# Product with V split over four quarters of the TensorE array, with scores and mask packed to the 64x64 blocks that are kept

## The chip, the cores and the metric

The kernel runs on one core of one Trainium2 chip. The metric is the device time of one execution in microseconds, the median of several runs.

## The reference

The input x has 16 sequences of 256 tokens with 256 features, 4096 tokens in all. A modulation computed from a small vector gives every sequence its shifts, gains and gates. The first half of the layer is a chunked linear attention with 16 heads of 128 features:

```python
h = layernorm(x) * (1 + ca) + sa
q, k, v = (h @ w.T + b for each of the three weights), 16 heads of D = 128
qn, kn = q and k divided by their norms; gv = softplus(h @ b_w.T + b_b) * v
attn = einsum('bnhid,bnhjd->bnhij', qn, kn)       # inside chunks of C = 64 tokens only
mask = where(j <= i, 1, 0)                        # the decay is exp(0) wherever the mask keeps
out = einsum('bnhij,bnhjd->bnhid', attn * mask, gv)
out = (out * silu(h @ og_w.T)) @ o_w.T + o_b
x = x + ga * out
```

The second half is a mixture of 16 experts (top 6 of them by a softmax) and a shared expert on all tokens, added to x with the gate gb.

## The kernel before

**Tiling.** Tokens lie in 32 tiles of 128, in 8 "supertiles" of 512 tokens. The heads lie in 4 groups of 4. The attention part is a loop of N = 128 steps, one for each pair of token tile and head group (`for n in range(N + 2)` at L928 on TensorE and L1507 on VectorE); four steps (t = 0 to 3) make a supertile with one head group. The expert part is a second loop, of 100 units (`for u in range(2, NU)`, L973), in which nothing of the change occurs.

**One step on TensorE, in order.** `project(i, t, Q)`, side tasks, `project(i, t, K)`, at t = 2 half of the output projection of the previous supertile, `score(n - 1)`, `project(i, t, V)`, the other half of the output projection, `attend(n - 1)`, `turn(n)`, more side tasks, and at t = 1 the four gate products. Side tasks are small pieces of other stages (norms, routing, preparing weights) placed by `plan()` (L68). A projection is six matmuls with a moving operand of 512 columns in the reduced fp32r format (`split_product`, L647: high and low parts of both operands, two halves of the contraction). `turn` (L838) transposes Q and K of the step, four matmuls each.

**Scores.** A 128-token tile has two chunks of 64 tokens, c = 0 and 1. `score` (L855) makes for each head and chunk the 64x64 block k.T @ q: contraction over the 128 features, 64 output partitions (the tokens j), 64 columns (the tokens i). Chunk c goes to output partitions 64c to 64c+63 and to columns 64c to 64c+63 of the head's 128, so that a head fills the two diagonal blocks of a 128x128 square in the PSUM bank `s_ps`. Its off-diagonal blocks are not written by these products. All operands are full fp32, for which the program has two pairs of weight load and matmul for each call.

**Mask.** On VectorE, `mask` (L1431) multiplies the whole bank, 128 partitions by 512 columns, by `causal` (128x128, broadcast over the four heads) into `scores`. `causal` is built once by GpSimd (L576 to L585): an upper triangle of ones with the upper right 64x64 block set to zero.

**Product with V.** `attend` (L869) makes for each head out = v.T @ scores with the whole array: contraction over 128 tokens, 128 output partitions (the features), 128 columns, into the PSUM bank `av_ps`. It waits for the mask, for V scaled by GpSimd (`v_scaled`) and for `gated_done` of the step before, which says that `av_ps` was read.

**After it.** On VectorE, `apply_gate` (L1443) multiplies `av_ps` by the gate into `gated`; ScalarE and VectorE split `gated` into a high and a low part for the output projection. `add_bias(n, V)` (L1421) on VectorE waits for `attended`, because it overwrites a V buffer; so do the copies of turned Q and K on ScalarE wait for `scored`.

**PSUM.** All eight banks are in use: two for projections, `qt_ps`, `kt_ps`, `s_ps`, `av_ps`, `out_ps`, `misc`. In the expert part `s_ps` and `av_ps` hold sums of experts; `down` (L906) waits for `masked` and `gated_done` of the last step before it.

Of the kernel before, what the change touches and what calls it, by code (L numbers as in the profile page):

```python
# [6 lines left out]
ALU = mybir.AluOpType  # L7
# [3 lines left out]
P = 128  # L11
# [12 lines left out]
HG = 4  # L24
NG = NH // HG
CH = 64
# [12 lines left out]
Q, K, V, G, O = range(5)  # L39
# [7 lines left out]
def after(eng, sem, count):  # L47
    if count > 0:
        eng.wait_ge(sem, count)
# [6 lines left out]
def heads(ap):  # L56
    return ap.rearrange("p (h d) -> p h d", d=P)
# [77 lines left out]
def build(nc, x, q_w, q_b, k_w, k_b, v_w, v_b, b_w, b_b, og_w, o_w, o_b, gate_w, w13, w2, sw13, sw2, c, wmod, out):  # L135
    ctx = ExitStack()
    with ctx:
        sb = lambda name, shape, dt=FP32: ctx.enter_context(nc.sbuf_tensor(name, shape, dt))
# [15 lines left out]
        beta = sb("beta", [P, NT, NH])  # L154
        minus_half = sb("minus_half", [P, 2 * HG])
        primed = sb("primed", [P, 1])
        causal = sb("causal", [P, P])


        w_qkv = sb("w_qkv", [P, 2, 3, KC, 2, 512], F32R)  # L160
# [3 lines left out]
        raw = [[sb(f"{n}_sb{b}", [P, HG * P]) for b in range(2)] for n in "qkv"]  # L164
# [3 lines left out]
        inv_norm = [sb(f"inv_norm{b}", [P, 2 * HG]) for b in range(2)]  # L168
        v_scale = [sb(f"v_scale{b}", [P, HG]) for b in range(2)]
        q_t, k_t = sb("q_t", [P, HG * P]), sb("k_t", [P, HG * P])  # L170
        scores = sb("scores", [P, HG * P])
        gate = sb("gate", [P, HG, ST])
        gated = [sb(f"gated{b}", [P, HG, P]) for b in range(2)]
        gated_hi, gated_lo = sb("gated_hi", [P, HG, ST], F32R), sb("gated_lo", [P, HG, ST], F32R)
# [37 lines left out]
        boot_ps = [qt_ps, kt_ps, s_ps, av_ps, qt_ps, kt_ps, s_ps, av_ps, av_ps, qt_ps]  # L212
        boot_before = [0, 0, 0, 0, 1, 2, 3, 4, 8, 0]
        late_wmod = [[work[:, 0:512], work[:, 512:1024]], [acc[:, 1, 0:512], acc[:, 1, 512:1024]]]
        y_ps = [[qt_ps, kt_ps], [s_ps, av_ps]]
        g_ps, u_ps = proj_ps[0], [proj_ps[1], out_ps]

# [354 lines left out]
        @block.gpsimd  # L572
        def _(pool):
            pool.memset(ident, 0.0)
            pool.memset(minus_half[:, :], -0.5)
            pool.memset(causal[:, :], 1.0)  # L576
            pool.memset(prob_ext[:, :, E:E + 2], 2.0).then_inc(made, 1)
            pool.wait_ge(made, 1)
            pool.affine_select(out=ident, in_=ident, compare_op=ALU.not_equal, fill=1.0, base=0,
                               pattern=[[-1, P]], channel_multiplier=1)  # L580
            pool.affine_select(out=causal[:, :], in_=causal[:, :], compare_op=ALU.is_ge, fill=0.0, base=0,
                               pattern=[[1, P]], channel_multiplier=-1).then_inc(made, 1)
            pool.wait_ge(made, 2)
            pool.memset(causal[0:CH, CH:P], 0.0).then_inc(made, 1)
            pool.wait_ge(made, 3)  # L585

            def do(task):
                if task[0] == "stats":
                    v = norm_at[task[1:3]]
                    pool.wait_ge(eps_added, v + 1)  # L590
                    after(pool, xn_done, v)
                    pool.tensor_tensor(rstd[:, :], var_eps[:, :], minus_half[:, 0:TS], ALU.pow).then_inc(rstd_done, 1)
                elif task[0] == "tile" and task[1] == NM - 2 and task[2] == 0:
                    u = nat_at["tile", NM - 1]
                    pool.wait_ge(nat_turned, u - 1)
                    pool.memset(nat[u % 2][:, :], 0.0).then_inc(nat_padded, 1)

            for task in boot:
                do(task)
            for n in range(N):  # L600
                i, t = divmod(n, TS)
                b, s, g = t % 2, supertile(i), group(i)
                for task in side[n, 0]:
                    do(task)
                pool.wait_ge(guard_done, n + 1)
                after(pool, q_scaled, n - 1)
                after(pool, scale_done, n - 1)
                pool.tensor_tensor(inv_norm[b][:, :], guarded[b][:, :], minus_half[:, :], ALU.pow).then_inc(inverted, 1)  # L608
                pool.wait_ge(inverted, n + 1)
                q = heads(raw[Q][b][:, :])  # L610
                pool.tensor_tensor(q, q, inv_norm[b][:, 0:HG].unsqueeze(2).broadcast_to([P, HG, P]), ALU.mult)\  # L611
                    .then_inc(q_scaled, 1)
                after(pool, v_scaled, n - 1)
                pool.wait_ge(beta_ready, s + 1)
                pool.tensor_tensor(v_scale[b][:, :], inv_norm[b][:, HG:2 * HG],
                                   beta[:, s * TS + t, g * HG:(g + 1) * HG], ALU.mult).then_inc(scale_done, 1)
                pool.wait_ge(scale_done, n + 1)
                pool.wait_ge(biased[V], n + 1)
                v = heads(raw[V][b][:, :])
                pool.tensor_tensor(v, v, v_scale[b][:, :].unsqueeze(2).broadcast_to([P, HG, P]), ALU.mult)\  # L620
                    .then_inc(v_scaled, 1)
                for task in side[n, 1]:
                    do(task)
            for u in range(NU):
                for task in late[u]:
                    do(task)
# [1 line left out]

        @block.tensor
        def _(pe):  # L630
            pe.wait_ge(made, 3)


            ORDER = [(w, t) for t in range(2) for w in (Q, K, V)] + [("gate", h) for h in range(HG)] + \
# [220 lines left out]
            def score(n):  # L855
                pe.wait_ge(qt_copied, n)
                pe.wait_ge(kt_copied, n)
                after(pe, masked, n - 1)
                if n == 1:
                    pe.wait_ge(gained, 3)  # L860


                for h in range(HG):
                    for c in range(P // CH):
                        at = slice(h * P + c * CH, h * P + (c + 1) * CH)
                        mm = pe.matmul(s_ps[c * CH:(c + 1) * CH, at], k_t[:, at], q_t[:, at], start=True, stop=True)  # L866
                mm.then_inc(scored, 1)

            def attend(n):  # L869
                pe.wait_ge(masked, n)  # L870
                pe.wait_ge(v_scaled, n)
                after(pe, gated_done, n - 1)
                if n == 1:
                    pe.wait_ge(boot_lo, 10)
                for h in range(HG):
                    at = slice(h * P, (h + 1) * P)
                    mm = pe.matmul(av_ps[:, at], raw[V][(n - 1) % 2][:, at], scores[:, at], start=True, stop=True)  # L877
                mm.then_inc(attended, 1)


# [318 lines left out]
        def _(dve):  # L1199
# [196 lines left out]
            def late_modulation():  # L1396
                dve.wait_ge(mod_turned, 2)
                dve.tensor_copy(mod[:, 4:12, :], s_ps[:, 2 * P:4 * P].rearrange("p (r d b) -> p r d b", r=8, d=2)[:, :, 0, :])\
                   .then_inc(gained, 1)
                dve.wait_ge(made, 3)  # L1400
                dve.wait_ge(gained, 3)
                gain = mod[:, CB * KC:(CB + 1) * KC, :]
                dve.tensor_scalar(gain, gain, 1.0, None, ALU.add).then_inc(gained, 1)
                steps = 4
                for w in (GA, GB):
                    m, s = mod[:, w * KC:(w + 1) * KC, :], sign[:, :, :]
                    dve.wait_ge(gained, steps)
                    dve.tensor_scalar(s, m, 0.0, 2.0, ALU.is_ge, ALU.mult).then_inc(gained, 1)
                    dve.wait_ge(gained, steps + 1)
                    dve.scalar_tensor_tensor(out=m, in0=m, scalar=-1.0, in1=m, op0=ALU.mult, op1=ALU.max).then_inc(gained, 1)  # L1410
                    dve.wait_ge(gained, steps + 2)
                    dve.tensor_scalar(m, m, 0.25, None, ALU.max).then_inc(gained, 1)
                    dve.wait_ge(gained, steps + 3)
                    dve.scalar_tensor_tensor(out=m, in0=s, scalar=-1.0, in1=m, op0=ALU.add, op1=ALU.mult).then_inc(gained, 1)
                    steps += 4
                dve.wait_ge(gained, steps)
                for h in range(KC):
                    dve.tensor_scalar(ga_ob[:, h, :], mod[:, GA * KC + h, :], o_b_sb[:, h:h + 1], None, ALU.mult)\
                       .then_inc(gained, 1)
# [11 lines left out]
            def mask(n):  # L1431
                dve.wait_ge(scored, n)
                after(dve, attended, n - 1)
                dve.tensor_tensor(heads(scores[:, :]), heads(s_ps[:, :]),
                                  causal[:, :].unsqueeze(1).broadcast_to([P, HG, P]), ALU.mult).then_inc(masked, 1)

            def sum_squares(n):
                dve.wait_ge(q_squared, n + 1)
# [4 lines left out]
            def apply_gate(n):  # L1443
                i, t = divmod(n - 1, TS)
                dve.wait_ge(attended, n)
                dve.wait_ge(gate_ready, HG * (i + 1))
                after(dve, gated_hi_done, n - 2)
                after(dve, gated_lo_done, n - 2)
                dve.tensor_tensor(gated[t % 2][:, :, :], heads(av_ps[:, :]), gate[:, :, t * P:(t + 1) * P], ALU.mult)\
                   .then_inc(gated_done, 1)  # L1450

            def lo_part(n):
                i, t = divmod(n - 1, TS)
# [133 lines left out]
```

## Time and profile before

| | us |
|---|---|
| median of 3 runs | 2165.3 (2164.62 to 2166.77) |
| the profiled execution | 2164.84 |
| its span in the trace | 2163.1 |
| TensorE busy | 2135.4 (99%) |
| VectorE busy | 1154.5 (53%) |
| ScalarE busy | 1031.5 (48%) |
| GpSimd busy | 522.2 (24%) |

The profiled execution took 0.5 us less than the median, and its span lacks 1.7 us of its time. In the profile PE is TensorE's matmul side and PEld its weight loads, which overlap the matmuls; DVE is VectorE, ACT ScalarE, POOL GpSimd. The end of a matmul is modelled and lies after the start of the next one, so consecutive matmuls overlap in these rows: what a block of matmuls costs is read from its start to the start of the next block, not from its busy time. `x8` on a row is the number of instructions merged in it.

### The profile page before, as it was taken

The page shows a single profiled execution, that of the slowest core. Times are in us where ns is not written, and L with a number is a line of the kernel's source. Part 1 is how long each engine was busy: PE and PEld are TensorE (multiplying, and loading weights), DVE is VectorE, ACT ScalarE, POOL GpSimd, SP SyncE. Part 2 cuts the span into 40 slices and gives each one's busy share as a digit, 9 for nine tenths or more (in the row PEclk, how much of TensorE's full clock was granted, in tenths as well). Part 3 has the DMA queues.
Part 4 walks back from the last instruction along what each step waited for, and adds up shares of the span by engine and source line. Part 5 has one row for each costly group of instructions (what it writes and reads, how often), then busy time and mean ns, then how long its engine had stood idle before and what let it go on. Part 6 is the DMA issues. An engine that isn't in the chain of part 4 may idle for free.

```text
span 2163.1 us, 36173 instructions
## 1 busy us (share of the span) xinstructions
PE 2135.4 (99%) x12463; PEld 1752.6 (81%) x12463; DVE 1154.5 (53%) x2174; ACT 1031.5 (48%) x3300; POOL 522.2 (24%) x540
## 2 busy tenths in 40 slices
PE   8999999999999999999999999999999999999999
PEld 6778888888888887878888888888888888888887
DVE  6555654555555555555554445555555455545554
ACT  6655664665665665565565453333332333333232
POOL 2433443443443343343343441000000000000000
PEclk9999999999999999999999999999999999999999
DMA  8574443254355354354233221342334234323221
GB/s 264 185 239 133 146 138 123 81 162 139 93 145 159 84 154 136 95 147 142 106 143 113 70 107 49 129 170 98 127 125 149 88 121 156 103 97 113 96 94 63
DMA packets 191892, 274.79 MB, mean 127 GB/s; under 512 B 99184, under 2 KB 132960, under 8 KB 191712
## 3 DMA queue, kind: packets, MB, share of 16 engines
q1 hardware_dynamic: 191712, 272.49, 39.6%
q8 instruction: 101, 1.65, 0.3%
q14 instruction: 79, 0.65, 0.1%
HBM read 214.79 MB, written 57.67 MB: 126 GB/s over the span
## 4 chain that ended last, share of the span: by engine, by line
PE 92%; DVE 3%; ACT 2%; issue 2%; DMA 1%; DVEq 0%; POOL 0%; SPq 0%; ACTq 0%; POOLq 0%
PE proj_ps L651 49%; PE out_ps L651 14%; PE av_ps L877 5%; PE s_ps L866 4%; PE s_ps L924 3%; PE av_ps L924 3%; PE qt_ps L924 3%; PE kt_ps L924 3%; PE qt_ps L847 2%; PE kt_ps L852 2%; DMA head_scr<-stage 1%; PE misc_ps L670 1%; PE out_ps L721 0%; ACT squares L1117 0%; PE misc_ps L679 0%
## 5 line engine op out<-in xcount | busy, mean ns | idle before, releaser
L651 PE MATMUL proj_ps<-w_qkv,h_t 128*128 128x512 f32 x2304 | 618.0, 406 | 10.3 <-DVE q_sb L1428 2.1
L651 PEld LDWEIGHTS proj_ps<-w_qkv,h_t 128*128 128x128 f32 x2304 | 407.9, 188 | 103.3 <-issue 20.2
L651 PE MATMUL proj_ps<-h_t,w_qkv 128*128 128x512 f32 x1800 | 444.2, 391 | 0.3 <-issue 0.2
L651 PEld LDWEIGHTS proj_ps<-h_t,w_qkv 128*128 128x128 f32 x1800 | 335.6, 188 | 70.2 <-issue 1.3
L608 POOL TENSOR_TENSOR inv_norm<-guarded,minus_half 128x8 f32<-128x8 f32 x128 | 209.4, 1636 | 741.9 <-DVE guarded L1441 741.9
L1108 ACT ACTIVATE q_t<-qt_ps 128x512 f32<-128x512 f32 x128 | 76.3, 596 | 303.9 <-PE qt_ps L847 303.4
L651 PE MATMUL proj_ps<-h_t,w_gate 128*128 128x512 f32 x768 | 190.2, 398 | 2.6 <-ACT gate L1131 1.3
L1428 DVE TENSOR_TENSOR v_sb<-proj_ps,bias 128x512 f32<-128x512 f32 x128 | 88.5, 691 | 190.0 <-PE av_ps L877 183.4
L1117 ACT ACTIVATE squares<-q_sb 128x128 f32<-128x128 f32 x512 | 151.4, 297 | 56.9 <-DVE q_sb L1428 52.4
L1428 DVE TENSOR_TENSOR q_sb<-proj_ps,bias 128x512 f32<-128x512 f32 x128 | 88.4, 690 | 165.5 <-PE proj_ps L651 160.7
L651 PEld LDWEIGHTS proj_ps<-h_t,w_gate 128*128 128x128 f32 x768 | 139.8, 188 | 40.2 <-ACT gate L1131 10.7
L1117 ACT ACTIVATE squares<-k_sb 128x128 f32<-128x128 f32 x512 | 151.1, 297 | 19.8 <-DVE k_sb L1428 18.2
L651 PE MATMUL out_ps<-gated_hi,w_out 128*128 128x512 f32 x512 | 158.0, 390 | 0.1
L651 PE MATMUL out_ps<-h_t,w_qkv 128*128 128x512 f32 x594 | 150.9, 389 | 0.0
L1428 DVE TENSOR_TENSOR k_sb<-proj_ps,bias 128x512 f32<-128x512 f32 x128 | 88.4, 690 | 116.1 <-PE proj_ps L651 115.7
L877 PEld LDWEIGHTS av_ps<-scores,v_sb 128*128 128x128 f32 x1024 | 133.9, 191 | 10.7
L1151 ACT ACTIVATE w_gate<-v_sb 128x512 fp32r<-128x512 f32 x100 | 63.2, 632 | 161.8 <-DVE v_sb L1499 161.8
L1151 ACT ACTIVATE w_gate<-squares 128x512 fp32r<-128x512 f32 x100 | 63.2, 632 | 158.8 <-DVE squares L1499 154.6
L620 POOL TENSOR_TENSOR v_sb<-v_sb,v_scale 128x512 f32<-128x512 f32 x128 | 135.6, 1059 | 10.0
L611 POOL TENSOR_TENSOR q_sb<-q_sb,inv_norm 128x512 f32<-128x512 f32 x128 | 135.2, 1056 | 10.0
L877 PE MATMUL av_ps<-scores,v_sb 128*128 128x128 f32 x1024 | 134.7, 274 | 0.0
L651 PEld LDWEIGHTS out_ps<-h_t,w_qkv 128*128 128x128 f32 x594 | 111.5, 188 | 23.5
(216 smaller groups left out, 3174.5 us busy)
## 6 DMA issues: line engine op xcount, KB each, us to landing
w_qkv<-tile_scr SPq DMA_DIRECT2D x100, 768.0 KB, 4.3
w_qkv<-head_scr SPq DMA_DIRECT2D x45, 1024.0 KB, 11.0
head_scr<-stage SPq DMA_DIRECT2D x30, 512.0 KB, 3.8
w_gate<-head_scr SPq DMA_DIRECT2D x15, 1024.0 KB, 4.9
w_out<-head_scr SPq DMA_DIRECT2D x15, 1024.0 KB, 4.9
tile_scr<-stage SPq DMA_DIRECT2D x25, 512.0 KB, 3.1
x_in<-_attn_hidden_states_dram SPq DMA_DIRECT2D x16, 512.0 KB, 6.7
h_scr<-stage SPq DMA_DIRECT2D x16, 512.0 KB, 3.3
```

The lines of the kernel that those rows point to most:

```text
L608: pool.tensor_tensor(inv_norm[b][:, :], guarded[b][:, :], minus_half[:, :], ALU.pow).then_inc(inverted, 1)
L611: pool.tensor_tensor(q, q, inv_norm[b][:, 0:HG].unsqueeze(2).broadcast_to([P, HG, P]), ALU.mult)\
L620: pool.tensor_tensor(v, v, v_scale[b][:, :].unsqueeze(2).broadcast_to([P, HG, P]), ALU.mult)\
L651: mm = pe.matmul(out, w, y, start=(j == 0 and m == 0), stop=(3 * j + m == n - 1))
L847: mm = pe.transpose(qt_ps[:, h * P:(h + 1) * P], raw[Q][b][:, h * P:(h + 1) * P], ident)
L866: mm = pe.matmul(s_ps[c * CH:(c + 1) * CH, at], k_t[:, at], q_t[:, at], start=True, stop=True)
L877: mm = pe.matmul(av_ps[:, at], raw[V][(n - 1) % 2][:, at], scores[:, at], start=True, stop=True)
L924: mm = pe.matmul(y_ps[a][h][:, :], tiles_w[:, w % 4, r, at], y, start=(m == 0 and j == 0), stop=(m == NM - 1 and j == 2))
L1108: act.activation(q_t[:, :], qt_ps[:, :], ACT.Copy).then_inc(qt_copied, 1)
L1117: m = act.activation(squares[:, what, at], raw[what][n % 2][:, at], ACT.Square, accum_out=sumsq[n % 2][:, what * HG + h:what * HG + h + 1])
L1151: act.activation(hid_hi[u % 2], hid[u % 2], ACT.Copy).then_inc(hid_hi_done, 1)
L1428: dve.tensor_tensor(raw[what][t % 2][:, :], proj_ps[at][:, :], bias[:, (i // 2) % 2, what, :], ALU.add)\
```

## The change

`score` puts both chunks of a head in the same 64 columns (partitions 0 to 63 and 64 to 127), so that the scores of four heads fill 256 columns and `s_ps` has its second half free. `causal` becomes two 64x64 triangles one above the other. The mask works on 256 columns. `attend` makes, for each head, half d of V's 64 columns and chunk c, a 64x64 product with contraction over 64 tokens; chunk 0 writes `av_ps`, chunk 1 the second half of `s_ps`. The gate is applied by two instructions, one for each chunk. `score` waits for `gated_done` of the step before.

```diff
--- before.py
+++ after.py
@@ -154,7 +154,7 @@
         beta = sb("beta", [P, NT, NH])
         minus_half = sb("minus_half", [P, 2 * HG])
         primed = sb("primed", [P, 1])
-        causal = sb("causal", [P, P])
+        causal = sb("causal", [P, CH])
 
 
         w_qkv = sb("w_qkv", [P, 2, 3, KC, 2, 512], F32R)
@@ -168,7 +168,7 @@
         inv_norm = [sb(f"inv_norm{b}", [P, 2 * HG]) for b in range(2)]
         v_scale = [sb(f"v_scale{b}", [P, HG]) for b in range(2)]
         q_t, k_t = sb("q_t", [P, HG * P]), sb("k_t", [P, HG * P])
-        scores = sb("scores", [P, HG * P])
+        scores = sb("scores", [P, HG * CH])
         gate = sb("gate", [P, HG, ST])
         gated = [sb(f"gated{b}", [P, HG, P]) for b in range(2)]
         gated_hi, gated_lo = sb("gated_hi", [P, HG, ST], F32R), sb("gated_lo", [P, HG, ST], F32R)
@@ -212,6 +212,8 @@
         boot_ps = [qt_ps, kt_ps, s_ps, av_ps, qt_ps, kt_ps, s_ps, av_ps, av_ps, qt_ps]
         boot_before = [0, 0, 0, 0, 1, 2, 3, 4, 8, 0]
         late_wmod = [[work[:, 0:512], work[:, 512:1024]], [acc[:, 1, 0:512], acc[:, 1, 512:1024]]]
+
+        attended_ps = [av_ps[:, 0:HG * CH], s_ps[:, HG * CH:2 * HG * CH]]
         y_ps = [[qt_ps, kt_ps], [s_ps, av_ps]]
         g_ps, u_ps = proj_ps[0], [proj_ps[1], out_ps]
 
@@ -577,12 +579,14 @@
             pool.memset(prob_ext[:, :, E:E + 2], 2.0).then_inc(made, 1)
             pool.wait_ge(made, 1)
             pool.affine_select(out=ident, in_=ident, compare_op=ALU.not_equal, fill=1.0, base=0,
-                               pattern=[[-1, P]], channel_multiplier=1)
-            pool.affine_select(out=causal[:, :], in_=causal[:, :], compare_op=ALU.is_ge, fill=0.0, base=0,
-                               pattern=[[1, P]], channel_multiplier=-1).then_inc(made, 1)
+                               pattern=[[-1, P]], channel_multiplier=1).then_inc(made, 1)
             pool.wait_ge(made, 2)
-            pool.memset(causal[0:CH, CH:P], 0.0).then_inc(made, 1)
+            pool.affine_select(out=causal[0:CH, :], in_=causal[0:CH, :], compare_op=ALU.is_ge, fill=0.0, base=0,
+                               pattern=[[1, CH]], channel_multiplier=-1).then_inc(made, 1)
             pool.wait_ge(made, 3)
+            pool.affine_select(out=causal[CH:P, :], in_=causal[CH:P, :], compare_op=ALU.is_ge, fill=0.0, base=0,
+                               pattern=[[1, CH]], channel_multiplier=-1).then_inc(made, 1)
+            pool.wait_ge(made, 4)
 
             def do(task):
                 if task[0] == "stats":
@@ -628,7 +632,7 @@
 
         @block.tensor
         def _(pe):
-            pe.wait_ge(made, 3)
+            pe.wait_ge(made, 4)
 
 
             ORDER = [(w, t) for t in range(2) for w in (Q, K, V)] + [("gate", h) for h in range(HG)] + \
@@ -856,14 +860,15 @@
                 pe.wait_ge(qt_copied, n)
                 pe.wait_ge(kt_copied, n)
                 after(pe, masked, n - 1)
+
+                after(pe, gated_done, n - 1)
                 if n == 1:
                     pe.wait_ge(gained, 3)
-
 
                 for h in range(HG):
                     for c in range(P // CH):
                         at = slice(h * P + c * CH, h * P + (c + 1) * CH)
-                        mm = pe.matmul(s_ps[c * CH:(c + 1) * CH, at], k_t[:, at], q_t[:, at], start=True, stop=True)
+                        mm = pe.matmul(s_ps[c * CH:(c + 1) * CH, h * CH:(h + 1) * CH], k_t[:, at], q_t[:, at], start=True, stop=True)
                 mm.then_inc(scored, 1)
 
             def attend(n):
@@ -872,9 +877,16 @@
                 after(pe, gated_done, n - 1)
                 if n == 1:
                     pe.wait_ge(boot_lo, 10)
+
+
                 for h in range(HG):
-                    at = slice(h * P, (h + 1) * P)
-                    mm = pe.matmul(av_ps[:, at], raw[V][(n - 1) % 2][:, at], scores[:, at], start=True, stop=True)
+                    to = slice(h * CH, (h + 1) * CH)
+                    for d in range(P // CH):
+                        for c in range(P // CH):
+                            rows, cols = slice(c * CH, (c + 1) * CH), slice(d * CH, (d + 1) * CH)
+                            mm = pe.matmul(attended_ps[c][cols, to],
+                                           raw[V][(n - 1) % 2][rows, h * P + d * CH:h * P + (d + 1) * CH],
+                                           scores[rows, to], start=True, stop=True)
                 mm.then_inc(attended, 1)
 
 
@@ -1397,7 +1409,7 @@
                 dve.wait_ge(mod_turned, 2)
                 dve.tensor_copy(mod[:, 4:12, :], s_ps[:, 2 * P:4 * P].rearrange("p (r d b) -> p r d b", r=8, d=2)[:, :, 0, :])\
                    .then_inc(gained, 1)
-                dve.wait_ge(made, 3)
+                dve.wait_ge(made, 4)
                 dve.wait_ge(gained, 3)
                 gain = mod[:, CB * KC:(CB + 1) * KC, :]
                 dve.tensor_scalar(gain, gain, 1.0, None, ALU.add).then_inc(gained, 1)
@@ -1431,8 +1443,9 @@
             def mask(n):
                 dve.wait_ge(scored, n)
                 after(dve, attended, n - 1)
-                dve.tensor_tensor(heads(scores[:, :]), heads(s_ps[:, :]),
-                                  causal[:, :].unsqueeze(1).broadcast_to([P, HG, P]), ALU.mult).then_inc(masked, 1)
+                dve.tensor_tensor(scores[:, :].rearrange("p (h n) -> p h n", n=CH),
+                                  s_ps[:, 0:HG * CH].rearrange("p (h n) -> p h n", n=CH),
+                                  causal[:, :].unsqueeze(1).broadcast_to([P, HG, CH]), ALU.mult).then_inc(masked, 1)
 
             def sum_squares(n):
                 dve.wait_ge(q_squared, n + 1)
@@ -1446,8 +1459,11 @@
                 dve.wait_ge(gate_ready, HG * (i + 1))
                 after(dve, gated_hi_done, n - 2)
                 after(dve, gated_lo_done, n - 2)
-                dve.tensor_tensor(gated[t % 2][:, :, :], heads(av_ps[:, :]), gate[:, :, t * P:(t + 1) * P], ALU.mult)\
-                   .then_inc(gated_done, 1)
+                for c in range(P // CH):
+                    m = dve.tensor_tensor(gated[t % 2][:, :, c * CH:(c + 1) * CH],
+                                          attended_ps[c].rearrange("p (h n) -> p h n", n=CH),
+                                          gate[:, :, t * P + c * CH:t * P + (c + 1) * CH], ALU.mult)
+                m.then_inc(gated_done, 1)
 
             def lo_part(n):
                 i, t = divmod(n - 1, TS)
```

## Rows read from the trace of the kernel before

**Rows 1.** The page, engines and granted clock in 40 slices.

```profile
PE 2135.4 (99%) x12463; PEld 1752.6 (81%) x12463; DVE 1154.5 (53%) x2174; ACT 1031.5 (48%) x3300; POOL 522.2 (24%) x540
...
PEclk9999999999999999999999999999999999999999
```

**Rows 2.** The page, chain that ended last, by line.

```profile
PE proj_ps L651 49%; PE out_ps L651 14%; PE av_ps L877 5%; PE s_ps L866 4%; PE s_ps L924 3%; PE av_ps L924 3%; PE qt_ps L924 3%; PE kt_ps L924 3%; PE qt_ps L847 2%; PE kt_ps L852 2%; DMA head_scr<-stage 1%; PE misc_ps L670 1%; PE out_ps L721 0%; ACT squares L1117 0%; PE misc_ps L679 0%
```

**Rows 3.** Groups by form, PE: out<-in, shapes, count | busy us, mean ns | idle before.

```profile
L877 PE MATMUL av_ps<-scores,v_sb 128*128 128x128 f32 x1024 | 134.7, 274 | 0.0
L866 PE MATMUL s_ps<-q_t,k_t 128*64 128x64 f32 x2048 | 87.7, 228 | 0.0
```

**Rows 4.** Timeline of PE in one step: start us, duration us, what.

```profile
806.41 0.69 PE L866 MATMUL s_ps<-q_t,k_t 128*64 128x64 f32 x16
807.02 1.66 PE L651 MATMUL proj_ps<-w_qkv,h_t 128*128 128x512 f32 x6
808.52 1.05 PE L877 MATMUL av_ps<-scores,v_sb 128*128 128x128 f32 x8
809.41 0.60 PE L847 MATMUL qt_ps<-ident,q_sb 128*128 128x128 f32 x4
...
812.02 3.25 PE L651 MATMUL proj_ps<-h_t,w_gate 128*128 128x512 f32 x11 [0.20 <-DVE v_sb L1428]
```

**Rows 5.** The same timeline in narrow windows, single matmuls around both blocks.

```profile
806.08 0.40 PE L651 MATMUL proj_ps<-w_qkv,h_t 128*128 128x512 f32 x1
...
806.41 0.28 PE L866 MATMUL s_ps<-q_t,k_t 128*64 128x64 f32 x2
...
806.87 0.22 PE L866 MATMUL s_ps<-q_t,k_t 128*64 128x64 f32 x1
...
807.36 0.39 PE L651 MATMUL proj_ps<-w_qkv,h_t 128*128 128x512 f32 x1
...
808.29 0.39 PE L651 MATMUL proj_ps<-w_qkv,h_t 128*128 128x512 f32 x1
```

**Rows 6.** Timeline of PE, the block of `beta`: four strips of 32 array columns.

```profile
206.29 0.65 PE L679 MATMUL misc_ps<-h_f,small_wt 128*32 128x128 f32 x16
...
206.66 0.27 PE L679 MATMUL misc_ps<-h_f,small_wt 128*32 128x128 f32 x1
```

**Rows 7.** Narrow windows: transposes after a wait, and in a running stream.

```profile
925.99 0.20 PEld L670 LDWEIGHTS misc_ps<-ident,xn 128*128 128x128 f32 x2 [0.33 <-issue]
...
926.15 0.49 PE L670 MATMUL misc_ps<-ident,xn 128*128 128x128 f32 x3
...
809.52 0.49 PE L847 MATMUL qt_ps<-ident,q_sb 128*128 128x128 f32 x3
```

**Rows 8.** Groups of DVE by line.

```profile
L1434 DVE TENSOR_TENSOR scores<-s_ps,causal 128x512 f32<-128x512 f32 x128 | 88.3, 690 | 1.9 <-PE s_ps L866 1.9
L1449 DVE TENSOR_TENSOR gated<-av_ps,gate 128x512 f32<-128x512 f32 x128 | 87.5, 683 | 0.7 <-PE av_ps L877 0.4
...
L1210 DVE BATCH_NORM_STATS2 stats<-x_in 128x6 f32<-128x256 f32 x64 | 22.4, 412 | 5.0 <-DMA x_in<-_attn_hidden_states_dram 5.0
```

**Rows 9.** Timelines of DVE and PE: the shortest distance from gate to score.

```profile
1315.27 0.68 DVE L1449 TENSOR_TENSOR gated<-av_ps,gate 128x512 f32<-128x512 f32 x1
...
1317.08 0.69 PE L866 MATMUL s_ps<-q_t,k_t 128*64 128x64 f32 x16
```

**Rows 10.** Waits: who <- for whom: us in total, times, longest us.

```profile
PEld s_ps L866 <- issue: 45.8, 128, 0.4
...
PEld proj_ps L651 <- ACT gate L1131: 10.7, 20, 0.8
...
PEld proj_ps L651 <- DVE v_sb L1428: 2.6, 6, 0.6
```

**Rows 11.** Timeline of the first microseconds.

```profile
2.06 0.14 POOL L584 MEMSET causal<- 64x64 f32 x1
...
6.01 0.36 PE L746 MATMUL proj_ps<-ident,q_t 16*128 16x16 f32 x2 [6.01 <-ACT q_t L1076]
```

## The prediction

> **What bounds the kernel now.** I read the page first. TensorE is busy 99% of the span and every slice has its full granted clock, while VectorE is busy about half the time [rows 1]. The chain that ended last says the same: its large entries are all TensorE's, with the product with V (L877) at 5% and the scores (L866) at 4% [rows 2]. So time taken off TensorE's own stream in the 128 attention steps should come off the end nearly one for one, and nothing else in this change can bring much. The groups give the sizes [rows 3]: L877 has 1024 matmuls, 8 a step (4 heads, two passes each for fp32); L866 has 2048, 16 a step. Busy times overlap, so I price every block from its start to the start of the next one.
>
> **The product with V now.** In the step shown the block begins at 808.52 and the transposes behind it at 809.41 [rows 4]: 0.89 us, 0.111 us for each full-array matmul of 128 columns. In front of it the last fp32r matmul starts 0.23 us earlier (808.29) [rows 5], and the first transpose is followed by the second after 0.11 us (809.41 to 809.52) [rows 4, 7]. From the last V projection to the second transpose: 0.23 + 0.89 + 0.11 = 1.23 us.
>
> **The product with V after.** It becomes 4 heads x 2 halves x 2 chunks x 2 passes = 32 matmuls, each 64 rows by 64 array columns, 64 moving columns. No row shows the array cut in its rows. The nearest are the scores, cut in two column strips, and the `beta` block, cut in four.
> - The scores' 16 matmuls run from 806.41 to 806.87, first to last start [rows 4, 5]: 0.46 us. One such matmul needs about 0.05 us for its 64 columns (a 128-column matmul is listed with 0.27 us [rows 6], a 64-column one with 0.22 [rows 5]). One after another 15 of them would take 0.8 us, so two strips do run at once: 8 rounds of two, about 0.06 us a round.
> - The 16 `beta` matmuls of 128 columns (about 0.1 us each by the same reckoning) start within 206.29 to 206.66, 0.37 us [rows 6]. One at a time 15 would take 1.5 us, two at a time 0.8; 0.37 is four at a time. So four strips run at once although each call puts its two passes one behind the other on the same strip.
> - If quarters behave like strips, the new block is again 8 rounds, of four matmuls instead of two. I take 0.46 us, and 0.01 us for two more starts in the last round (my estimate).
>
> **What cutting the array costs.** Only the scores change the tiling now, at both ends, and the trace shows its price. The weight loader stands idle for 0.36 us (45.8/128) before every one of the 128 score blocks, released by nothing but "issue" [rows 10]: the load isn't pulled ahead of running matmuls there. Last K matmul to first score is 0.33 us (806.08 to 806.41) where entering the product with V takes 0.23 [rows 4, 5]. Last score to first V matmul is 0.15 us, and the second V matmul comes 0.34 us behind the first (807.02 to 807.36) [rows 4, 5], about 0.1 more than the 0.23 usual for such a matmul, since its weights were not loaded ahead. Behind the new block come transposes: after a wait, from the first load (925.99) to the second transpose (926.15) is 0.16 us [rows 7], against 0.11 in a running stream.
>
> Sum after: 0.33 + 0.46 + 0.01 + 0.15 + 0.16 = 1.11 us. Saved: 0.12 us a step, 128 times: 15.4 us. The sum is against the profiled execution (2164.84, span 2163.1), which stands 0.5 us under the median; I take it off the median: 2165.3 - 15.4 = 2149.9, say **2150**.
>
> The Trainium skill, "TensorEngine Tiling (Array Packing)", Key Properties, says that changing the tiling mode drains the engine; that agrees with the 0.36 us above, and it speaks against this change, which adds a third mode between two full-array blocks. By the page's ideal of a factor of four the block alone would be 0.22 us, and the sum 0.25 us a step or 32 us better than mine (2118); the strips in the rows stay a good way short of such a factor, and I go by them.
>
> **The other parts.**
> - *Scores*: same count, same shapes, only other output columns: nothing.
> - *Mask*: 690 ns for 512 columns now [rows 8]. A VectorE instruction on 256 columns takes 412 ns [rows 8], so 0.28 us less a step; *gate*: two of about 0.41 instead of one of 683 ns, 0.14 more. VectorE gains 0.14 us a step and mostly waits for TensorE. It matters only where TensorE waits for it: at 812.02 the gate products stand 0.20 us for the V bias [rows 4], and all such stalls on V's bias are 2.6 us, those on ScalarE's gate 10.7 us [rows 10]. The mask lies ahead of the V bias in VectorE's queue, so that stall rather shrinks (up to 2 us gained). For ScalarE's, TensorE arrives sooner in 32 of the steps: at worst 32 x 0.12 = 4 us not gained. I take zero for both.
> - *The wait moved forward*: `score` waits for `gated_done` of the step before, which `attend` needed anyway, two blocks later. Behind it on TensorE stand the scores and all that follows; who needs them is the mask. Where it is shortest in the trace the gate ends at 1315.95 and the next scores start at 1317.08 [rows 9]: 1.1 us of slack against 0.14 us more gate. Nothing, and if it were late by 0.1 us everywhere, 13 us.
> - *`attend`'s own wait*: between the scores' end and the product with V lie six matmuls, 1.50 us (807.02 to 808.52) [rows 4], and the mask that must fit in there gets shorter. Nothing.
> - *Constants*: GpSimd's last one ends at 2.2 us, the new pair some 0.5 us later (estimate from its 0.14 us now), and TensorE's first instruction is at 6.01 us, held by ScalarE [rows 11]. No queue of DMAs is touched. Nothing.
> - *Program size*: 3072 more matmuls (4096 for 1024 [rows 3]) and as many loads, on 12463 of each [rows 1]. Nothing shown waits for instructions now, so I take nothing, unless the sequencer can't deliver 64 instructions in half a microsecond, which is the second rival below.
> - *Expert part*: the extra waits are long past there. Nothing.
>
> **Bounds of the unknown cost.** The new block could be as short as 0.46 with the exit cheaper by 0.05, and 2 us gained through VectorE: 0.17 x 128 = 22, plus 2, gives 2141. With rounds of 0.07 instead of 0.06 us the saving is 0.04 us a step and the time 2160.
>
> **Rivals.**
> 1. *The row halves don't overlap (slower).* The two chunks of one half of V's columns share array columns, and if loads or streams of the upper and lower rows go one behind the other, the 32 matmuls take 16 rounds of two. Eight more rounds of 0.06 are 0.48 us; net 0.36 us a step worse, 46 us: 2211. For it: no row of this kernel shows row halves at work. Against it: column strips show that matmuls of separate parts do overlap, two passes and all, and chunks write separate banks. It decides from 0.12/8 = 0.015 us more a round, that is from 0.075 us.
> 2. *A least spacing of matmuls.* Averaged, `beta` starts one each 25 ns (0.37/15) [rows 6], the scores one each 31 ns (0.46/15) [rows 4, 5], and nothing in the trace is faster. If 25 ns is a limit of the stream, 32 matmuls need 0.78 us, 0.31 more than I have: 0.19 us a step worse than now, 24 us, 2190; at 31 ns it comes to about 2212. For it: both blocks sit near one average though their work differs. Against it: each average is already explained by columns per round, and the first two scores start 0.01 us apart (two of 0.27 us within 0.28) [rows 5]. The Trainium skill, "TensorE: Matmul & The Clock Gate", Part 1, has a rule of just this kind, that start-to-start never drops below about 25 ns however small the matmul; its Part 3 has about 4 ns between tiles.
> 3. *Gained and lost (same).* The rounds are four matmuls with four loads; at 0.07 to 0.08 us each, or with a costlier drain behind four quarters, the two edges (0.10 in front, 0.04 + 0.05 behind) eat the gain: 2161 to 2170.
>
> **How the numbers follow.** A difference of 0.2%, 4.3 us, is about what a measurement of this kernel can tell from none: faster is below 2161, slower above 2169.6. My sum as it stands, 2140 to 2160: 0.70, with the chance beyond it on the good side 0.01. Rival 3: 0.10, of it 0.08 within 0.2% and 0.02 slower, up to 2175. Rival 1: 0.12. Rival 2: 0.07. That makes faster 0.71, same 0.08, slower 0.21. The range 2140 to 2175 leaves out rivals 1 and 2 and the rest, 0.2 together. Likeliest is the sum, 2150.
>
> **What would show it.** In the profile after: PE at L877 with 4096 matmuls of 64x64; from its first to its last start 0.45 to 0.50 us (rival 1: about 0.95; rival 2: 0.8 or more); from the block's start to the transposes 0.6 to 0.65; PEld idle with "issue" before L877, 128 times, about 0.36 us, and a smaller idle before L847; the last V matmul 0.33 us ahead of the block instead of 0.23. Mask groups at about 415 ns, gate 256 of about 415 ns. No wait of L866 for the gate. The clock stays full; a lower one in any slice would make the forecast wrong for another reason, as would a wait of TensorE for instructions.

## The result, and the profile after

| | us | ratio to the kernel before |
|---|---|---|
| changed kernel, median of 4 runs | 2152.05 (2149.9 to 2153.89) | 0.9939, 95% interval 0.9922 to 0.9956 |
| kernel before, same runs | 2164.96 | 1 |
| changed kernel once more, 5 runs (control) | 2152.31 (2150.42 to 2153.0) | 0.9937, 0.9925 to 0.9950 |

The change makes the kernel 13 to 14 us faster. The profiled execution took 2149.9 us with a span of 2148.2, against 2163.1 before. First the page of the changed kernel, its engines and the granted clock, which answer to [rows 1]:

```profile
PE 2119.0 (99%) x15535; PEld 1692.9 (79%) x15535; DVE 1131.6 (53%) x2302; ACT 1028.7 (48%) x3300; POOL 525.8 (24%) x540
...
PEclk9999999999999999999999999999999999999999
```

TensorE is still the bound, at full clock, with 3072 more matmuls. The groups of the product with V by form, which answer to [rows 3] (L887 is the new product, L871 the scores):

```profile
L887 PE MATMUL av_ps<-scores,v_sb 64*64 64x64 f32 x2048 | 88.1, 224 | 0.0
L887 PE MATMUL s_ps<-scores,v_sb 64*64 64x64 f32 x2048 | 88.1, 224 | 0.0
L871 PE MATMUL s_ps<-q_t,k_t 128*64 128x64 f32 x2048 | 87.7, 228 | 0.0
```

Each chunk of the new product is busy 88.1 us with its 2048 matmuls, as the scores are with theirs, though the two chunks take turns in the program. That is the first sign that they run side by side. The timeline shows it directly. These are narrow windows around one block, start and duration in us, which answer to [rows 4, 5]:

```profile
785.07 0.40 PE L655 MATMUL proj_ps<-w_qkv,h_t 128*128 128x512 f32 x1
785.40 0.27 PE L887 MATMUL av_ps<-scores,v_sb 64*64 64x64 f32 x1
785.41 0.27 PE L887 MATMUL s_ps<-scores,v_sb 64*64 64x64 f32 x1
785.41 0.27 PE L887 MATMUL av_ps<-scores,v_sb 64*64 64x64 f32 x1
785.42 0.27 PE L887 MATMUL s_ps<-scores,v_sb 64*64 64x64 f32 x1
785.51 0.22 PE L887 MATMUL av_ps<-scores,v_sb 64*64 64x64 f32 x1
...
785.57 0.22 PE L887 MATMUL av_ps<-scores,v_sb 64*64 64x64 f32 x1
...
785.88 0.22 PE L887 MATMUL s_ps<-scores,v_sb 64*64 64x64 f32 x1
786.03 0.65 PE L851 MATMUL qt_ps<-ident,q_sb 128*128 128x128 f32 x4
...
786.19 0.38 PE L851 MATMUL qt_ps<-ident,q_sb 128*128 128x128 f32 x2
```

Four matmuls start within 0.02 us (785.40 to 785.42), two into each bank; the next four follow from 785.51, and from there a round of four comes every 0.06 us. The block's starts span 0.48 us. From the last V projection to the second transpose it is 0.33 + 0.63 + 0.16 = 1.12 us, where it was 1.23: 0.11 us saved, 128 times, which is 14 us, the size of the result. The step shown stands for all: the same distances over 127 steps of both traces average 1.229 us before and 1.116 after, 14.5 us in 128 steps, of the 14.9 us by which the two spans differ.

The waits of the weight loader (who <- for whom: us in total, times, longest), which answer to [rows 10]:

```profile
PEld av_ps L887 <- issue: 46.3, 128, 0.4
PEld s_ps L871 <- issue: 45.9, 128, 0.4
...
PEld proj_ps L655 <- ACT gate L1143: 10.1, 20, 0.8
...
PEld proj_ps L655 <- DVE v_sb L1440: 1.7, 6, 0.5
```

The second tiling has the same signature as the first: 0.36 us of idle loader before each block, with no other engine named. The waits for ScalarE's gate and for V's bias on VectorE are 11.8 us together, against 13.3 in [rows 10]. And the groups of VectorE, which answer to [rows 8]:

```profile
L1446 DVE TENSOR_TENSOR scores<-s_ps,causal 128x256 f32<-128x256 f32 x128 | 54.3, 424 | 1.8 <-PE s_ps L871 1.8
L1463 DVE TENSOR_TENSOR gated<-av_ps,gate 128x256 f32<-128x256 f32 x128 | 53.4, 417 | 1.8 <-PE s_ps L887 1.0 <-issue 0.4
L1463 DVE TENSOR_TENSOR gated<-s_ps,gate 128x256 f32<-128x256 f32 x128 | 52.9, 413 | 0.0
```

By their durations mask and gate take 1.25 us a step where they took 1.37, 15 us less in all. VectorE's busy time falls by more, from 1154.5 to 1131.6 us, since the rows of consecutive VectorE instructions overlap.

### The profile page after: what moved, and what is told of

Same layout as the page of the kernel before. It is cut to its first block, busy times and chain, and to the rows that moved or that the text cites. A ratio compares the mean times of both kernels' runs of the same rounds, so it can differ in the third digit from the quotient of the medians.

```text
span 2148.2 us, 42572 instructions
## 1 busy us (share of the span) xinstructions
PE 2119.0 (99%) x15535; PEld 1692.9 (79%) x15535; DVE 1131.6 (53%) x2302; ACT 1028.7 (48%) x3300; POOL 525.8 (24%) x540
## 4 chain that ended last, share of the span: by engine, by line
PE 93%; DVE 3%; ACT 2%; DMA 1%; issue 1%; SPq 0%; DVEq 0%; ACTq 0%
PE proj_ps L655 50%; PE out_ps L655 14%; PE s_ps L871 4%; PE s_ps L936 3%; PE qt_ps L851 3%; PE av_ps L936 3%; PE qt_ps L936 3%; PE kt_ps L936 3%; PE av_ps L887 3%; PE kt_ps L856 2%; DMA head_scr<-stage 1%; PE s_ps L887 1%; PE misc_ps L674 1%; PE out_ps L725 0%; ACT squares L1129 0%
## 5 line engine op out<-in xcount | busy, mean ns | idle before, releaser
L655 PEld LDWEIGHTS proj_ps<-h_t,w_gate 128*128 128x128 f32 x768 | 139.8, 188 | 39.0 <-ACT gate L1143 10.1
L615 POOL TENSOR_TENSOR q_sb<-q_sb,inv_norm 128x512 f32<-128x512 f32 x128 | 137.5, 1074 | 10.1
L1158 ACT ACTIVATE q_sb<-proj_ps 128x512 f32<-128x512 f32 x100 | 59.7, 597 | 119.2 <-PE proj_ps L655 119.2
L1158 ACT ACTIVATE k_sb<-proj_ps 128x512 f32<-128x512 f32 x100 | 59.7, 597 | 118.2 <-PE proj_ps L655 118.2
```

Source lines behind the costliest of these rows:

```text
L655: mm = pe.matmul(out, w, y, start=(j == 0 and m == 0), stop=(3 * j + m == n - 1))
L1158: act.activation(silu_g[u % 2][:, :], g_ps[:, :], ACT.Silu).then_inc(silu_done, 1)
```

## The experiments

Two questions were open behind a right number. Is the gain all TensorE's, as the sum had it? And why do quarters overlap, what does an edge cost, and what would the other cuts have given? All times are medians; differences to the changed kernel are taken to 2152.3 (control). Each group ran beside the kernel before on one chip (2166.2, 2165.4 and 2166.0).

**Control.** The changed kernel unaltered.

> The changed kernel once more, beside the others on the same chip: 2150 to 2154 us, about 13 us under the kernel before.

Measured 2152.31, as expected.

### Is the gain all TensorE's?

**Packing alone.** The array is whole again in the product with V, `scores` is 128 x 512 again with its other blocks zeroed once, the mask is two instructions by rows (64 partitions of each chunk), and the gate is one instruction as before:

```diff
+pool.memset(scores[:, :], 0.0)
...
 def attend(n):
...
+    at = slice(h * P, (h + 1) * P)
+    mm = pe.matmul(av_ps[:, at], raw[V][(n - 1) % 2][:, at], scores[:, at], start=True, stop=True)
...
 def mask(n):
...
+    for c in range(P // CH):
+        rows = slice(c * CH, (c + 1) * CH)
+        m = dve.tensor_tensor(heads(scores[rows, :])[:, :, c * CH:(c + 1) * CH],
+                              s_ps[rows, 0:HG * CH].rearrange("p (h n) -> p h n", n=CH),
+                              causal[rows, :].unsqueeze(1).broadcast_to([CH, HG, CH]), ALU.mult)
...
```

> Scores and mask are packed as in the change, but the product with V stays on the whole array (the mask writes two diagonal blocks into scores zeroed once; the gate is one instruction again). My theory, that the whole gain is TensorE's shorter block and its edges: no gain, 2165 us, within 4 of the kernel before, and TensorE's block at 0.89 us again. Rival, that the smaller mask or the emptier bank brings a part of the gain: 2155 to 2160 us.

Measured 2172.58, ratio 1.0031 (1.0019 to 1.0042): 6.4 us slower than the kernel before. TensorE's block is the old one; what changed is that the mask is two instructions:

```profile
L1444 DVE TENSOR_TENSOR scores<-s_ps,causal 64x256 f32<-64x256 f32 x256 | 107.9, 422 | 3.5 <-PE s_ps L872 1.9
```

Half the partitions save nothing, 422 ns each, 0.84 us a step instead of 0.69, and VectorE's busy time is 1189.6 us, 35 more than in the kernel before. TensorE's block is at 0.89 us in every step, so the packing leaves it alone, as my theory had it, but 35 us more of VectorE cost 6 us, which it had at none. Whether a mask that is really smaller would give something by itself this run can't tell, since its mask is not smaller. In this kernel's waits TensorE's loader stands for V's bias on VectorE 7.7 us (2.6 in [rows 10]) and for ScalarE's gate 14.0 (10.7).

**Mask twice.**

```diff
+for to in (spare, scores):
+    m = dve.tensor_tensor(to[:, :].rearrange("p (h n) -> p h n", n=CH),
...
+m.then_inc(masked, 1)
```

> The changed kernel with the mask made twice (the first time into a spare buffer): 0.42 us more of VectorE in each of 128 steps, 53 us of work. My theory, that VectorE lies off the chain except for a few steps with gate products: 0 to 3 us more than the changed kernel, 2152 to 2155. Rival, that its relief was a term of the result: 8 us more or above.

Measured 2158.14, 5.8 us more than the control: above both ends that I gave my theory, under the rival's 8. VectorE's busy time is 1171.0 us, 39 more than in the changed kernel, and the loader's waits, 10.1 and 1.7 us there, are longer:

```profile
PEld proj_ps L655 <- ACT gate L1143: 12.1, 20, 0.9
...
PEld proj_ps L655 <- DVE v_sb L1440: 3.7, 6, 0.8
```

VectorE is not clear of the chain, but much more work on it costs little.

**VectorE's load put back.** One small instruction ahead of the mask:

```diff
+scores, spare = sb("scores", [P, HG * CH]), sb("spare", [P, 8])
...
 def mask(n):
...
+    dve.tensor_tensor(spare[:, :], causal[:, 0:8], causal[:, 0:8], ALU.mult)
...
```

> The changed kernel with one more small VectorE instruction (128x8, 0.16 us) ahead of each mask: VectorE's work in a step is then about that of the kernel before (0.42 + 0.83 + 0.16 against 0.69 + 0.68). What it costs over 2152 is VectorE's share in the gain. After the two runs that missed (packing alone 6 us slower with 0.15 us more of VectorE a step, mask twice 6 us slower with 0.42): 1 to 4 us, 2153 to 2156. If VectorE's relief was no part of the gain: 2152.

Measured 2157.94 (2157.07 to 2159.2, against 2150.42 to 2153.0 of the control): 5.6 us more, above the expected 1 to 4. The instruction stands behind the mask's waits. The page says that VectorE now has about the load of the kernel before, 1148.8 us against 1154.5, though not in the same places (mask shorter, gate longer than there):

```profile
PE 2123.6 (98%) x15535; PEld 1692.2 (78%) x15535; DVE 1148.8 (53%) x2430; ACT 1031.7 (48%) x3300; POOL 524.5 (24%) x540
```

```profile
PEld proj_ps L655 <- ACT gate L1143: 12.3, 20, 1.7
...
PEld proj_ps L655 <- DVE v_sb L1440: 2.9, 7, 0.7
```

Read by the time alone, 2166.0 - 2157.9 = 8 us would be the shorter block's and the other 5.6 VectorE's. The groups of TensorE by form say otherwise. The first line is the control, the second this run:

```profile
L655 PE MATMUL out_ps<-gated_hi,w_out 128*128 128x512 f32 x512 | 158.1, 390 | 0.1
L655 PE MATMUL out_ps<-gated_hi,w_out 128*128 128x512 f32 x512 | 160.7, 395 | 0.1
```

The 512 matmuls of the output projection that read `gated_hi` take 395 ns instead of 390, and the 256 that read `gated_lo` 394 instead of 389 (100.9 us busy instead of 99.7), without a longer wait. That makes 3.8 us, and they are not work of VectorE's. In the kernel before, in the changed kernel and with the mask made twice they take 390 and 389 ns. What this run alone has is a buffer of 8 elements a partition (`spare`, 32 bytes) that is allocated ahead of theirs, so that they lie 32 bytes further on; the 256 elements of the doubled mask do no harm. That their place is the cause is likely, but no run tests it.

So this run is no clean measure of VectorE's share. Less the 3.8 us, the medians leave it 1.8 us; the listed waits for the gate and V's bias, 15.2 us here against 11.1 in the control and 11.8 in the first profile, say 3 to 4. VectorE's relief is thus worth some 2 to 4 us of the 13 to 14. That also fits the mask made twice: 39 us more of VectorE cost 5.8 us there, which would make 2.5 us of the 17 here.

### Do the quarters run at once, and what sets a round?

**Chunk 1 left out.** The loop over chunks runs for c = 0 only; half of the attention output is stale.

```diff
-for c in range(P // CH):
+for c in range(1):
```

> The changed kernel with the products of chunk 1 (the lower row half) left out of the product with V: 16 matmuls instead of 32, so that half of the attention output is stale. If the two row halves run wholly at once, the other 16 filled no time of their own: block still 0.43 to 0.47 us first to last start, total within 3 us of the changed kernel. If the halves run one behind the other, the block shrinks to about 0.24 us and the total falls by about 30 us to 2122.

Measured 2149.07, 3.2 us under the control. The timeline, the 16 matmuls left and the transposes behind them:

```profile
783.19 0.68 PE L887 MATMUL av_ps<-scores,v_sb 64*64 64x64 f32 x16
783.80 0.66 PE L851 MATMUL qt_ps<-ident,q_sb 128*128 128x128 f32 x4
```

0.61 us to the transposes against 0.63 with all 32 (0.613 and 0.626 on average). Half of the products cost some 0.01 us a step. The rival of row halves one behind the other is out.

**The block twice.**

```diff
+for again in range(2):
+    for h in range(HG):
...
```

> The changed kernel with all 32 matmuls of the product with V issued twice, same data: 64 in a row, 128 instructions with their loads. Rounds of four: 8 more at 0.052 to 0.06 us, 0.42 to 0.48 us a step, 54 to 61 us: 2206 to 2213. If a least spacing of 25 ns or the supply of instructions is near, the second 32 take 0.8 us: about 2255.

Measured 2203.97 (ratio 1.0176), 51.7 us more, a little under the expected. In the trace the 64 matmuls start within 0.943 us in every step, against 0.477 for the 32: 8 more rounds take 0.466 us, 0.058 each, which makes 59.6 us in 128 steps. The pace is the expected one; 8 us of it don't reach the end. TensorE comes later and waits less: the loader's wait for ScalarE's gate falls from 10.1 to 7.0 us, and that for V's bias on VectorE, 1.7 us, is gone from the list.

Sixty-four matmuls in a row start 15 ns apart on average, so neither a spacing of 25 ns nor the delivery of instructions binds, and the second rival is out too.

**One more change of tiling.** In `project`, ahead of K's products:

```diff
+if what == K and TS * i + t >= 2:
+    pe.matmul(ps[0:CH, 0:CH], ident[0:CH, 0:CH], ident[0:CH, 0:CH], start=True, stop=True)
```

> The changed kernel with one needless quarter product (64x64, two passes) ahead of each K projection, into columns that the projection overwrites: one more change of tiling and back in 126 steps. From the rows: 0.33 us from the last full matmul to it, 0.11 for its two passes, 0.15 to the next, 0.34 instead of 0.23 to the second, against 0.46: 0.45 us a step, 57 us, 2209. If a change of tiling costs nothing and only the matmuls count: 0.11 us a step, 14 us, 2166.

Measured 2198.07, 45.8 us more, 0.36 us each: two passes of a 64x64 product, some 0.12 us by the rounds above, cost three times that through their edges. It is under the expected 57. The loader's idle time before the added product tells a part of why:

```profile
PEld av_ps L889 <- issue: 46.4, 128, 0.4
PEld s_ps L873 <- issue: 45.9, 128, 0.4
PEld proj_ps L811 <- issue: 33.5, 126, 0.5
...
PEld proj_ps L655 <- issue: 9.0, 25, 0.7
```

It is 0.27 us there against 0.36, and the projection's own "issue" fell from 21.4 us (61 times) in the changed kernel to 9.0 (25): where TensorE had drained anyway, because it waits for its own transposes, the new tiling found it empty. The starts around the added product bear that out: it costs 0.45 us, as expected, where matmuls were running before it, and 0.25 us in the 35 steps where TensorE stood empty. That led to the last pair of runs.

**Row halves alone.** The product cut in two by its rows, over all 128 columns:

```diff
 for h in range(HG):
     to = slice(h * CH, (h + 1) * CH)
...
+    for c in range(P // CH):
+        rows = slice(c * CH, (c + 1) * CH)
+        mm = pe.matmul(attended_ps[c][:, to], raw[V][(n - 1) % 2][rows, h * P:(h + 1) * P],
+                       scores[rows, to], start=True, stop=True)
```

> The changed kernel with the product with V cut in row halves alone: 64 rows by all 128 array columns, 16 matmuls in 8 rounds of two. If a round is set by its weight load (128 columns, about 0.11 us by the exposed load of a full matmul): block 0.86 us, as long as before, plus the edges: 0.39 us a step more than the changed kernel, 50 us, 2202. If it is set by the 64 moving columns: 8 rounds of 0.053 to 0.058, no change, 2152.

Measured 2195.47, 43 us more (50 expected). Both chunks start together here as well, but a round takes 0.11 us:

```profile
803.10 0.27 PE L886 MATMUL av_ps<-scores,v_sb 64*128 64x64 f32 x1
803.11 0.27 PE L886 MATMUL s_ps<-scores,v_sb 64*128 64x64 f32 x1
803.21 0.27 PE L886 MATMUL av_ps<-scores,v_sb 64*128 64x64 f32 x1
803.22 0.27 PE L886 MATMUL s_ps<-scores,v_sb 64*128 64x64 f32 x1
```

The 64 moving columns are the same as in the quarters. What doubled is the width of the weights, 128 columns instead of 64, and the round doubled with it, to the 0.11 us that a full-array matmul of 128 moving columns takes in the kernel before. So the width sets the round here, and the streaming doesn't. That it does so through the weight load is the natural reading; no run separates the load from the wider output. Cutting the rows without the columns is slower than not cutting at all: 1.04 us to the transposes against 0.89. The block's 0.41 us a step would make 53 us; 10 of them don't reach the end, and again the waits are shorter (6.2 us for ScalarE's gate instead of 10.1).

### Does the order of the calls matter?

**Quarter by quarter.** The loop over heads innermost, the same 32 matmuls.

```diff
-for h in range(HG):
-    for d in range(P // CH):
-        for c in range(P // CH):
+for d in range(P // CH):
+    for c in range(P // CH):
+        for h in range(HG):
```

> The changed kernel with the loop over heads innermost: all eight passes of one quarter, then of the next, the same 32 matmuls. If every quarter has its own queue and the engine looks far ahead: the same time, 2152. If it looks ahead only a few matmuls, the quarters run mostly one after the other: 32 x 0.053 = 1.7 us for the block instead of 0.48, up to 156 us more, 2308; in between if it looks ahead part of the way.

Measured 2248.51 (ratio 1.0384), 96 us more, between the two ends expected. The timeline of one block; the program has eight passes into `av_ps`, eight into `s_ps`, and so on:

```profile
804.74 0.50 PE L887 MATMUL av_ps<-scores,v_sb 64*64 64x64 f32 x5
805.03 0.27 PE L887 MATMUL s_ps<-scores,v_sb 64*64 64x64 f32 x1
805.08 0.22 PE L887 MATMUL av_ps<-scores,v_sb 64*64 64x64 f32 x1
805.14 0.22 PE L887 MATMUL s_ps<-scores,v_sb 64*64 64x64 f32 x1
805.14 0.22 PE L887 MATMUL av_ps<-scores,v_sb 64*64 64x64 f32 x1
...
805.83 0.45 PE L887 MATMUL s_ps<-scores,v_sb 64*64 64x64 f32 x5
806.21 0.33 PE L851 MATMUL qt_ps<-ident,q_sb 128*128 128x128 f32 x1
```

Five matmuls of the first quarter start alone, for 0.29 us, before the first of the second quarter joins; then the two alternate, and the last five are alone again. The block takes 1.47 us to the transposes instead of 0.63. All 128 blocks have this order. So TensorE does start a matmul ahead of earlier ones that wait for their quarter, but only from a short way down its stream.

**Two heads a quarter.** In between: four passes of a quarter, then the next quarter.

```diff
+for d, c, h in ((d, c, 2 * pair + j) for pair in range(2) for d in range(2) for c in range(2) for j in range(2)):
...
```

> The same 32 matmuls, two heads (four passes) of one quarter in a row, then the next quarter. If TensorE can start matmuls that stand 12 places further on in its stream: block 0.48 us, 2152. If it sees only about six, as all quarters one after the other suggest: 0.6 to 1.0 us, 2170 to 2215.

Measured 2160.44, 8 us more, below what I gave the short view. Four matmuls still start within 0.04 us here, two into each bank, although the first pass of the fourth quarter stands 12 places behind; the block to the transposes takes 0.69 us instead of 0.63. So six places is too low a guess for how far ahead it sees; the exact depth is open.

### A version faster than both

In the kernel before and after, TensorE waits for its own transposes in two side tasks, only to signal that a buffer of natural weights is free. The signal can be had from the count of filled side banks. Both tasks ("prep" and "tile") and GpSimd's wait are changed in the same way as shown:

```diff
+nat_turned_by = lambda u: chunk_at[(*nat_order[u], 1)] + 1
...
 elif kind == "prep":
...
-    if h == KC - 1:
-        pe.wait_ge(side_filled, chunk_at[task] + 1)
-        pe.nop().then_inc(nat_turned, 1)
...
 def load_nat(t):
...
-    sp.wait_ge(nat_turned, u - 1)
+    sp.wait_ge(side_filled, nat_turned_by(u - 2))
```

> The changed kernel without TensorE's waits for its own transposes (two places in the side tasks): the loads of natural weights wait for the count of filled side banks instead. In the trace about 80 blocks of transposes are followed by the projection after 0.42 us instead of 0.03. If TensorE's stream is the end: up to 80 x 0.39 = 31 us less, 2121 to 2128. If other engines fill that time: under 10 us.

Measured 2142.32, ratio 0.9891 (0.9877 to 0.9905): 10 us less, not 31. The waits of the loader:

```profile
PEld proj_ps L656 <- ACT gate L1138: 11.1, 20, 1.0
PEld proj_ps L656 <- issue: 7.1, 22, 1.4
...
PEld proj_ps L656 <- DVE q_sb L1435: 3.4, 4, 1.5
```

"issue" before projections falls from 21.4 us (61) to 7.1 (22), 14 us: the edit removed some 40 drains, not 80, and the waits for VectorE and ScalarE, 12.3 us in these two rows after the change, are 14.5 now.

**The same on the kernel before.**

> The same edit on the kernel before: the two gains should add, so 2165 less the same 25 to 31 us, 2134 to 2140, and the ratio of the two edited kernels that of the two unedited ones, 0.994.

Measured 2153.46, ratio 0.9945 (0.9929 to 0.9961), 12.5 us less. 0.9891/0.9945 is 0.9946, beside 0.9937 for the change alone: within their intervals the two edits add. The expected 25 to 31 us went by the same wrong count of drains.

## Why the prediction was right, and where it was not

- **TensorE's path.** Term by term: into the block 0.33 us (0.33 forecast), block and exit 0.63 (0.62), first to second transpose 0.16 (0.16, taken there from the first load). Sum 1.12 against 1.11, saved 0.11 against 0.12. What made it come out was to price both edges from the scores, which already had them, and the overlap from the `beta` block, the one place that showed four at once.
- **Rival 1**, row halves one behind the other, is refuted: half of the products are worth some 0.01 us a step. **Rival 2**, a least spacing, is refuted: 32 matmuls in 0.48 us, 64 at the same pace. **Rival 3** was right that edges eat much of the gain, about 0.2 us a step, and wrong in the size of a round.
- **Scores, the wait moved forward, constants, program size at nothing.** No wait of the scores for the gate is listed after the change. TensorE's first wait, for ScalarE, is 6.2 us against 6.0; in the other runs of the changed kernel it lies between 5.6 and 6.5, so that says nothing of the constants.
- **VectorE and ScalarE at zero.** I wrote that at most 4 us would be lost because TensorE arrives sooner, and at most 2 gained from the shorter mask, and took zero for both. What they come to together can be read: the listed waits for the gate and V's bias went from 13.3 to 11.8 us, and outside the block and its edges the two profiled traces differ by 0.4 us; by the medians the gain is 0.6 to 1.6 us under the block's 14.5. So the zero held to within 2 us. What each is worth alone is less certain. The load put back gives 2 to 4 us for the relief, at or a little over my bound, once the slower output projection of that run is taken off; the loss is then some 2 to 5 us (14.5 by the block, 10 to 12 with VectorE no lighter). The two terms partly cancel, and I had no working for that: this part of the agreement is luck, but a matter of a few microseconds.
- **Expectations that missed.** The packing alone and the mask twice (up to 4 and 3 us expected, 6 measured each) I had with too little for VectorE's work. The load put back (1 to 4 expected, 5.6 measured) missed by the slower output projection. The block twice, row halves and one more change of tiling came out 2 to 11 us under what I expected. The pace of the first two and the 0.45 us of the third were right, but a longer block shortens other waits, and some changes of tiling fall where TensorE stands empty. The removed waits (up to 31 expected, 10 measured) had a wrong count.

## What to carry to other kernels

Let consecutive calls go to different parts of the array if small products are to run at once: eight passes of one quarter in a row cost 96 us here. With few moving columns cut the columns whenever the rows are cut, since here the width of the weights set the round. Price the two changes of tiling around each block: they took about 0.2 us, beside a block of 0.89, and a product worth 0.12 us, put between full-array blocks, cost 0.36. And when a run adds work to one engine to find that engine's share, compare the durations of all groups with the control before crediting the difference to it: the run here had 3.8 of its 5.6 us in matmuls that have nothing to do with VectorE.

## What the runs showed of the hardware that was not expected

- Matmuls of different quarters start out of program order: the first one into `s_ps`, ninth in the program, starts 0.29 us into the block while the sixth into `av_ps` comes later. The view ahead is limited: eight passes of one quarter in a row cost 96 us in all, four in a row 8 us.
- A VectorE instruction on 64 partitions by 256 columns takes 422 ns, as one on 128 partitions does (424 ns).
- With a 32-byte buffer allocated ahead of `gated_hi` and `gated_lo`, the 768 fp32r matmuls that read them take 395 and 394 ns instead of 390 and 389 (vector_as_before against control), 3.8 us in all. That the place in memory is the reason is not tested.
